# Self-attention on one core: four of sixteen key tiles a step added up by accumulating transfers instead of by TensorE and GpSimd

## The chip, the core and the metric

The kernel runs on one core of one Trainium2 chip. The metric is the device time of one execution in microseconds (us), taken as the median of several runs. One profiled execution stands beside it: it shows what each engine did, with every instruction's start and duration.

## What is computed

A transformer block pair: a cross-attention layer with residual, then a layer with self-attention, cross-attention and an MLP. The change touches the self-attention alone. Cut to that, the reference says:

```python
def mha(q, k, v):                       # B = 2, N = 2048, C = 512, 16 heads of d = 32
    scores = jnp.einsum('bqhd,bkhd->bhqk', qh, kh) / jnp.sqrt(jnp.asarray(d, q.dtype))
    attn = jax.nn.softmax(scores, axis=-1)
    out = jnp.einsum('bhqk,bkhd->bqhd', attn, vh)
    return out.reshape(B, Nq, C)

h = mha(q, k, v) @ self_o_w + self_o_b
x = x + h * gate_msa
```

All is float32 in and out. Every query's exponentials over 2048 keys have to be added up (the softmax's denominator), and this sum is what the change distributes anew.

## The kernel before

The program is a row of stages, each written by hand as one instruction list per engine with explicit semaphores: conditioning, a first cross-attention pass, the dense projections to q, k and v, the self-attention (`attention`, named a2, tiles a_...), a second cross-attention pass and the MLP. Nothing schedules it; the order is the order of the code.

The self-attention makes 32 steps: 2 batches, 4 groups of 4 heads (`GH`), 4 chunks of 512 queries (`W`). A step has 64 slots, x = 0 to 63: 16 key tiles kt of 128 keys times 4 heads. In slot x TensorE does `score_tile` (one score tile, keys on partitions, into a ring of three PSUM banks `st`), then the work that the hand-written table `products` gives to that slot, then `score_unit` (scores of a later step, queries on partitions, for their maxima). Around it:

- ScalarE takes each score tile out of `st` with an exponential into `e`, a ring of `ER` = 4 key tiles of [128 x 4 heads x 512] float32, 1 MB each. Before it writes tile kt it waits until TensorE has used the tile that stood in that place (`tile_used`) and, if GpSimd adds up that tile, until it has (`e_added`).
- VectorE takes the maximum of each `score_unit` (L1973). Once a step they are all there, it writes the negated maxima, GpSimd computes their lower parts (`lower_parts`, L2045), TensorE turns them (`turn_peaks`, L1807, in slot `TURN` - 1), ScalarE copies the rows (`take_rows`), and SP spreads them by a transfer into the next step's queries (`spread_rows`, L1738). The first score tile of the next step waits for that transfer.
- `weigh(kt)` (L1832) is four matmuls, one a head, that multiply the exponentials of key tile kt with the values and accumulate in `acc`, bank 0.
- The denominators accumulate in `acc`, bank 1, in one of two ways. A tile of `SUMMED` (3, 5, 8, 10, 15) is added by TensorE with a matrix of ones (`add_up`, four matmuls, L1841). The eleven tiles of `POOLED` are first added up element by element by GpSimd into `esum` (`add`, L2038, ten additions of 128 x 2048), and one `add_partial` (four matmuls, L1850) takes the sum in. The first addition of a step waits until TensorE is done with the sum of the step before; in before that is behind the products of slot 9.
- `fetch_sums` (ScalarE) takes both banks out, `divide` (VectorE, three parts) inverts the denominators, `scale` (GpSimd, L2051) multiplies, SP stores. The new step's `weigh(0)` waits for `fetch_sums`.

A matmul of `weigh` or of the sums is float32 in 32 columns and shows as two records of the trace, so such a call of four matmuls shows as x8. GpSimd's list for a step is: additions 1 to 7, `lower_parts` for the next step, addition 8, `scale` of the step before, additions 9 and 10. SP issues, per step: three query loads (L1720, `QR` = 4 buffers, three steps ahead), every fourth step key and value loads (L1728, L1732), the store of a finished chunk, and the spread of the rows. All transfers of the kernel before are issued by SP.

Of the kernel before, what the change touches and what calls it, by code (L numbers as in the profile page):

```python
# [13 lines left out]
P = 128  # L14
# [6 lines left out]
W = 512  # L21
# [1570 lines left out]
def attention(nc, d, name, q_in, k_in, v_in, o_out, keys, preload):  # L1592
# [30 lines left out]
    TURN = 60  # L1623
# [4 lines left out]
    DIVIDE_AT = (16, 24, 52)  # L1628
    FETCH_AT, SPREAD_AT = 9, 37
    SETUP = 2 + KW % 2  # L1630
    with nc.cleanup_on_exit(), ExitStack() as ctx:
# [12 lines left out]
        if POOLED:  # L1644
            esum = sb("esum", [P, GH, W])
        peak = sb("peak", [P, U])
# [3 lines left out]
        sums = sb("sums", [P, 2, 2, W])  # L1650
        den_t = sb("den_t", [P, W])
        inv = sb("inv", [P, W // DH])
        inv_b = sb("inv_b", [P, W])
        inv_t = sb("inv_t", [P, 2, W])
# [7 lines left out]
        score_done, score_read, tile_used, e_added = sem("score_done"), sem("score_read"), sem("tile_used"), sem("e_added")  # L1662
        divided, acc_read, scaled, spread = sem("divided"), sem("acc_read"), sem("scaled"), sem("spread")
# [120 lines left out]
        def _(pe):  # L1784
# [37 lines left out]
            def weigh(i, j, kt):  # L1822

                n, g = BODY * i + j, j // CHUNKS
                if kt == 0:
                    pe.wait_ge(acc_read, n + 1)
                    if j % CHUNKS == 0:
                        pe.wait_ge(v_loaded[g % 2], DMA * (i + g // 2 + 1))
                pe.wait_ge(score_read, number(i, j, place(kt, GH - 1)) + 3)
                for h in range(GH):  # L1830
                    rows = slice(h * DH, (h + 1) * DH)
                    mm = pe.matmul(acc[rows, 0], v[0:KR, g % 2, kt, rows], e[0:KR, (j * NKT + kt) % ER, h],  # L1832
                                   start=(kt == 0), stop=(kt == NKT - 1), tile_position=(0, h * DH))
                if kt in POOLED or kt in SUMMED_FIRST:
                    mm.then_inc(tile_used, 1)

            def add_up(i, j, kt):

                pe.wait_ge(score_read, number(i, j, place(kt, GH - 1)) + 3)
                for h in range(GH):  # L1840
                    mm = pe.matmul(acc[h * DH:(h + 1) * DH, 1], ones[0:KR], e[0:KR, (j * NKT + kt) % ER, h], start=(kt == SUMMED[0]),  # L1841
                                   stop=False, tile_position=(0, h * DH))
                if kt not in SUMMED_FIRST:
                    mm.then_inc(tile_used, 1)

            def add_partial(i, j):

                pe.wait_ge(e_added, (BODY * i + j + 1) * ADDS)
                for h in range(GH):
                    mm = pe.matmul(acc[h * DH:(h + 1) * DH, 1], ones[0:KR], esum[:, h], start=False, stop=True, tile_position=(0, h * DH))  # L1850

            def products(i, j, x):

                if x == 4 and exists(i, j - 1):
                    add_up(i, j - 1, 15)
                    weigh(i, j - 1, 14)
                elif x == 9 and exists(i, j - 1):
                    add_partial(i, j - 1)
                    weigh(i, j - 1, 15)
                elif x == 14 and exists(i, j):  # L1860
                    weigh(i, j, 0)
                elif x == 20 and exists(i, j):
                    weigh(i, j, 1)
                    weigh(i, j, 2)
                    weigh(i, j, 3)
                elif x == 25 and exists(i, j):
                    add_up(i, j, 3)
                elif x == 30 and exists(i, j):
                    weigh(i, j, 4)
                    add_up(i, j, 5)  # L1870
                    weigh(i, j, 5)
                elif x == 35 and exists(i, j):
                    weigh(i, j, 6)
                elif x == 40 and exists(i, j):
                    weigh(i, j, 7)
                elif x == 45 and exists(i, j):
                    weigh(i, j, 8)
                elif x == 50 and exists(i, j):
                    add_up(i, j, 8)
# [31 lines left out]
        def _(act):  # L1911
# [8 lines left out]
            def exponential(i, j, kt, h):  # L1920
                n = BODY * i + j
                if h == 0:
                    act.wait_ge(tile_used, n * NKT + kt + 1)
                    before = (kt - ER) % NKT
                    if before in POOLED and (kt >= ER or exists(i, j - 1)):

                        act.wait_ge(e_added, (n - (kt < ER)) * ADDS + max(POOLED.index(before), 1))
# [11 lines left out]
            def fetch_sums(i, j):  # L1939
                n = BODY * i + j  # L1940
                act.wait_ge(tile_used, (n + 1) * NKT + ER)
                act.wait_ge(scaled, n + 1)
                act.activation(sums[:, j % 2], acc[:], ACT.Copy).then_inc(acc_read, 1)
# [21 lines left out]
        def _(dve):  # L1965
# [19 lines left out]
            def divide(i, j, part):  # L1985
# [3 lines left out]
                if part == 0:  # L1989
                    dve.wait_ge(acc_read, n + 2)  # L1990
                    ins = dve.transpose(den_t[:], sums[:, j % 2, 1])
# [37 lines left out]
        def _(pool):  # L2029
# [17 lines left out]
            def scale(i, j):  # L2047
# [3 lines left out]
                pool.tensor_tensor(o[:, j % 2], sums[:, j % 2, 0], inv_t[:, j % 2], ALU.mult).then_inc(scaled, 1)  # L2051
# [256 lines left out]
```

## Time and profile before

| | us |
|---|---|
| median of 3 runs | 4050.16 (4046.61 to 4053.0) |
| the profiled execution | 4039.68 |
| its span, first to last instruction | 4037.9 |
| TensorE busy in the span | 3696.0 (92%) |
| VectorE, ScalarE, GpSimd busy | 2264.0, 1858.7, 2231.7 |
| first addition of the attention to its last `weigh` | 955.0 to 2683.3 |

A busy engine is one that has an instruction running; an idle stretch ahead of an instruction is put down to the engine or transfer that released it last. The span is cut by stage: the slices and the stretches in time order show the attention as one flat part with a period of one step. Within a step the times of the groups of TensorE and of GpSimd's additions can be subtracted from each other, and that is how the rows below are to be read.

### The profile page before, as it was taken

The page shows a single profiled execution, that of the slowest core. Times are in us where ns is not written, and L with a number is a line of the kernel's source. Part 1 is how long each engine was busy: PE and PEld are TensorE (multiplying, and loading weights), DVE is VectorE, ACT ScalarE, POOL GpSimd, SP SyncE. Part 2 cuts the span into 40 slices and gives each one's busy share as a digit, 9 for nine tenths or more (in the row PEclk, how much of TensorE's full clock was granted, in tenths as well). Part 3 has the DMA queues.
Part 4 walks back from the last instruction along what each step waited for, and adds up shares of the span by engine and source line. Part 5 has one row for each costly group of instructions (what it writes and reads, how often), then busy time and mean ns, then how long its engine had stood idle before and what let it go on. Part 6 is the DMA issues. An engine that isn't in the chain of part 4 may idle for free. (4 is left out here: it accounts for less than half of the span.)

```text
span 4037.9 us, 51412 instructions
## 1 busy us (share of the span) xinstructions
PE 3696.0 (92%) x19340; PEld 2421.3 (60%) x19340; DVE 2264.0 (56%) x3956; ACT 1858.7 (46%) x3431; POOL 2231.7 (55%) x987
## 2 busy tenths in 40 slices
PE   4699969979999999999999999958999949999998
PEld 2577748855545554555555555426777737888887
DVE  1466642228777777777777777614766634222222
ACT  1455641113666666666666666644556521111111
POOL 0356640004888888888888888864667542000000
PEclk8798889987999999999999999978999869999999
DMA  7556657773021312112131311024576651111110
GB/s 229 144 154 167 167 149 224 221 193 63 20 62 27 69 27 54 41 23 59 27 68 27 69 27 30 20 86 104 146 179 173 149 198 42 42 42 42 42 42 31
DMA packets 213509, 371.42 MB, mean 92 GB/s; under 512 B 36103, under 2 KB 52999, under 8 KB 209703
## 3 DMA queue, kind: packets, MB, share of 16 engines
q1 hardware_dynamic: 213287, 368.49, 33.6%
q8 instruction: 135, 2.21, 0.2%
q14 instruction: 87, 0.71, 0.1%
HBM read 215.54 MB, written 144.51 MB: 89 GB/s over the span
## 5 line engine op out<-in xcount | busy, mean ns | idle before, releaser
L1973 DVE TENSOR_REDUCE a_peak<-a_sm 128x1 f32<-128x512 f32 x2048 | 1263.5, 682 | 423.8 <-PE a_sm L1797 423.6
L2038 POOL TENSOR_TENSOR a_esum<-a_esum,a_e 128x2048 f32<-128x2048 f32 x288 | 1319.4, 4581 | 101.8 <-ACT a_e L1929 87.2
L1929 ACT ACTIVATE a_e<-a_st 128x512 f32<-128x512 f32 x2048 | 1063.7, 602 | 570.8 <-PE a_st L1819 476.1
L1797 PE MATMUL a_sm<-a_k,a_q 96*128 96x512 f32 x2048 | 875.6, 435 | 28.0 <-DMA a_k<-s_k 28.0
L1819 PE MATMUL a_st<-a_q,a_k 128*128 128x512 f32 x2048 | 826.3, 406 | 6.7 <-ACT a_e L1929 4.2
L1797 PEld LDWEIGHTS a_sm<-a_k,a_q 96*128 96x128 f32 x2048 | 394.3, 193 | 480.5 <-DVE a_peak L1973 267.7
L1832 PE MATMUL a_acc<-a_e,a_v 128*32 128x512 f32 x4096 | 515.7, 598 | 0.0
L1819 PEld LDWEIGHTS a_st<-a_q,a_k 128*128 128x128 f32 x2048 | 388.0, 190 | 116.7 <-ACT a_e L1929 41.6
L2169 PE MATMUL mlp_ph<-mlp_us,mlp_w_hi 128*128 128x512 f32 x1024 | 337.0, 391 | 32.6 <-DVE mlp_raw_lo L2218 32.6
L2211 ACT ACTIVATE mlp_gelu<-mlp_ph,mlp_b 128x512 f32<-128x512 f32 x128 | 88.1, 688 | 595.0 <-PE mlp_ph L2169 594.9
L2249 POOL TENSOR_TENSOR mlp_x<-mlp_x,mlp_brow 128x2048 f32<-128x2048 f32 x8 | 36.9, 4619 | 569.6 <-DMA mlp_x<-s_x 569.4
L2226 DVE CAST mlp_gs<-mlp_gelu 128x512 fp32r<-128x512 f32 x128 | 90.6, 708 | 459.2 <-ACT mlp_gelu L2211 459.2
L2184 PE MATMUL mlp_py<-mlp_w_hi,mlp_gs 128*128 128x512 f32 x1024 | 317.3, 391 | 16.7 <-DVE mlp_gs L2228 16.7
L1409 POOL TENSOR_TENSOR p_e<-p_e,p_inv 128x308 f32<-128x308 f32 x256 | 173.2, 709 | 167.1 <-DVE p_inv L1093 167.1
L1832 PEld LDWEIGHTS a_acc<-a_e,a_v 128*32 128x32 f32 x4096 | 110.2, 109 | 246.5 <-issue 159.5
L2169 PEld LDWEIGHTS mlp_ph<-mlp_us,mlp_w_hi 128*128 128x128 f32 x1024 | 193.7, 189 | 73.6 <-issue 33.0
L2184 PEld LDWEIGHTS mlp_py<-mlp_w_hi,mlp_gs 128*128 128x128 f32 x1024 | 191.6, 188 | 60.9 <-issue 16.1
L2038 POOL TENSOR_TENSOR a_esum<-a_e 128x2048 f32<-128x2048 f32 x32 | 146.9, 4591 | 130.9 <-PE a_acc L1832 115.4
L587 PE MATMUL p_sm<-p_ks,p_qs 96*128 96x78 f32 x1024 | 167.7, 306 | 50.1 <-DMA p_qs<-s_q 29.7
L587 PEld LDWEIGHTS p_sm<-p_ks,p_qs 96*128 96x128 f32 x1024 | 153.2, 217 | 82.2 <-issue 27.6
L2169 PE MATMUL mlp_ph<-mlp_us,mlp_raw_lo 128*128 128x512 f32 x512 | 200.3, 391 | 0.0
L2184 PE MATMUL mlp_py<-mlp_raw_lo,mlp_gs 128*128 128x512 f32 x512 | 199.9, 390 | 0.0
(150 smaller groups left out, 5167.7 us busy)
## 6 DMA issues: line engine op xcount, KB each, us to landing
p_qs<-s_q SPq DMA_DIRECT2D x192, 256.0 KB, 5.9
s_q<-p_qo SPq DMA_DIRECT2D x64, 512.0 KB, 7.4
a_q<-s_q SPq DMA_DIRECT2D x96, 256.0 KB, 5.2
a_k<-s_k SPq DMA_DIRECT2D x24, 1024.0 KB, 15.9
s_x<-p_x SPq DMA_DIRECT2D x16, 1024.0 KB, 4.3
s_u<-p_ut_hi SPq DMA_DIRECT2D x64, 256.0 KB, 5.8
s_u<-p_ut_lo SPq DMA_DIRECT2D x64, 256.0 KB, 6.4
p_us<-s_u SPq DMA_DIRECT2D x16, 1024.0 KB, 7.9
```

Of the source, the lines that this page charges most:

```text
L587: mm = pe.matmul(sm[:, unit % 2, h * KE:(h + 1) * KE], qs[0:3 * DH, g % 2, h, qt * P:(qt + 1) * P], ks[0:3 * DH, b, g * GH + h], start=Tru ...
L1409: pool.tensor_tensor(e[:, number % 2, qt, :, 0:S], e[:, number % 2, qt, :, 0:S], inv[:, number % 2, qt].unsqueeze(2).to_broadcast([P, GH, ...
L1797: mm = pe.matmul(sm[:, bank_of_unit(j, u), x * KE:(x + 1) * KE], q[0:3 * DH, j % QR, h, qt * P:(qt + 1) * P], k[0:3 * DH, g % 2, h, kc * K ...
L1819: pe.matmul(st[0:KR, place(kt, h) % RING], k[:, g % 2, h, kt * P:kt * P + KR], q[:, j % QR, h], start=True, stop=True).then_inc(score_done, 1)
L1832: mm = pe.matmul(acc[rows, 0], v[0:KR, g % 2, kt, rows], e[0:KR, (j * NKT + kt) % ER, h], start=(kt == 0), stop=(kt == NKT - 1), tile_posi ...
L1929: act.activation(e[0:KR, (j * NKT + kt) % ER, h], st[0:KR, place(kt, h) % RING], ACT.Exp, scale=SCALE).then_inc(score_read, 1)
L1973: dve.tensor_reduce(dst, src, AX.X, ALU.max).then_inc(unit_read, 1)
L2038: pool.tensor_tensor(esum[:], e[:, slot(0)] if x == 1 else esum[:], e[:, slot(x)], ALU.add).then_inc(e_added, 1)
L2169: mm = pe.matmul(ph[:, m % 4], w1[pw][:, t, m * P:(m + 1) * P], us[:, b, pm, t], start=(t == 0 and s == 0), stop=(t == KT - 1 and s == 2))
L2184: mm = pe.matmul(py[:, tt], gs[:, m % 2, pw, tt * P:(tt + 1) * P], w2[pm][:, m], start=(m == 0 and s == 0), stop=(m == HT - 1 and s == 2))
L2211: act.activation(gelu[:, m % 2], ph[:, m % 4], ACT.Gelu_apprx_tanh, bias=b1[:, m:m + 1]).then_inc(gelu_done, 1)
L2226: dve.tensor_copy(gs[:, m % 2, 0], gelu[:, m % 2]).then_inc(g_hi, 1)
```

## The change

The sixteen key tiles are distributed over three ways instead of two. GpSimd adds ten tiles (0, 1, 3, 4, 5, 7, 8, 10, 13, 14: nine additions), TensorE two (11 and 15), and four tiles (`MOVED`: 2, 6, 9, 12) are moved by transfers that GpSimd issues itself: tile 2 is copied from `e` to a second partial sum `esum_moved`, and 6, 9 and 12 are added to it by accumulating transfers of 1 MB each, every one waiting for the landing of the one before. A new `add_moved` (four matmuls) takes that sum in, at slot 14; GpSimd's first addition of a step now waits for it. ScalarE, before it writes a place of the ring that a moved tile held, waits for its transfer. The ring `e` grows to five tiles; to make room the query buffers go from 4 to 3, `sums` has one buffer instead of two, and `den_t` shares its place with `inv_b`. The product groups of TensorE move: ten groups, mostly six slots apart, instead of twelve, mostly five apart. The turn comes in slot 57 instead of 59, `fetch_sums` in slot 19 instead of 9, the three divisions at VectorE's 37, 48 and 51 instead of 16, 24 and 52.

```diff
-    QR = 4
-    ER = 4
-
-    POOLED = [0, 1, 2, 4, 6, 7, 9, 11, 12, 13, 14]
-    SUMMED = [3, 5, 8, 10, 15]
-    SUMMED_FIRST = [5, 10, 15]
+    QR = 3
+    ER = 5
+
+    POOLED = [0, 1, 3, 4, 5, 7, 8, 10, 13, 14]
+    MOVED = [2, 6, 9, 12]
+    SUMMED = [11, 15]
+    SUMMED_FIRST = [11, 15]
...
-    TURN = 60
+    TURN = 58
...
-    DIVIDE_AT = (16, 24, 52)
-    FETCH_AT, SPREAD_AT = 9, 37
+    DIVIDE_AT = (37, 48, 51)
+    FETCH_AT, SPREAD_AT = 19, 49
...
-                if kt in POOLED or kt in SUMMED_FIRST:
+                if (kt in POOLED or kt in MOVED or kt in SUMMED_FIRST) and kt < NKT - 1:
                     mm.then_inc(tile_used, 1)
...
+            def add_moved(i, j):
+
+                pe.wait_ge(e_moved, DMA * (BODY * i + j + 1) * len(MOVED))
+                for h in range(GH):
+                    mm = pe.matmul(acc[h * DH:(h + 1) * DH, 1], ones[0:KR], esum_moved[:, h], start=False, stop=True, tile_position=(0, h * DH))
+                mm.then_inc(tile_used, 1)
 
             def products(i, j, x):
 
-                if x == 4 and exists(i, j - 1):
+                if x == 2 and exists(i, j - 1):
+                    weigh(i, j - 1, 14)
                     add_up(i, j - 1, 15)
-                    weigh(i, j - 1, 14)
-                elif x == 9 and exists(i, j - 1):
+                    weigh(i, j - 1, 15)
+                elif x == 8 and exists(i, j - 1):
                     add_partial(i, j - 1)
-                    weigh(i, j - 1, 15)
-                elif x == 14 and exists(i, j):
+                elif x == 14 and exists(i, j - 1):
+                    add_moved(i, j - 1)
+                elif x == 22 and exists(i, j):
                     weigh(i, j, 0)
-                elif x == 20 and exists(i, j):
                     weigh(i, j, 1)
                     weigh(i, j, 2)
...
-                elif x == 55 and exists(i, j):
-                    add_up(i, j, 10)
                     weigh(i, j, 10)
+                    add_up(i, j, 11)
                     weigh(i, j, 11)
-                elif x == 63 and exists(i, j):
                     weigh(i, j, 12)
+                elif x == 60 and exists(i, j):
                     weigh(i, j, 13)
...
+                    if m >= 0 and before in MOVED:
+                        act.wait_ge(e_moved, DMA * (m * len(MOVED) + MOVED.index(before) + 1))
...
+            def move(i, j, y):
+
+                n, kt = BODY * i + j, MOVED[y]
+                pool.wait_ge(score_read, number(i, j, place(kt, GH - 1)) + 3)
+                if y == 0:
+                    pool.wait_ge(tile_used, n * NKT + ER)
+                    pool.dma_start(esum_moved[:], e[:, (j * NKT + kt) % ER]).then_inc(e_moved, DMA)
+                else:
+                    pool.wait_ge(e_moved, DMA * (n * len(MOVED) + y))
+                    pool.dma_start(esum_moved[:], e[:, (j * NKT + kt) % ER], accum_op=ALU.add).then_inc(e_moved, DMA)
 
             def step(i, j):
                 for x in range(1, len(POOLED)):
+                    if x == 2 and exists(i, j):
+                        move(i, j, 0)
+                    if x == 4 and exists(i, j):
+                        move(i, j, 1)
+                    if x == 6 and exists(i, j):
+                        move(i, j, 2)
+                    if x == 8 and exists(i, j):
+                        move(i, j, 3)
```

All the groups of `products` after the change, by slot: 2 (weigh 14, sum of 15, weigh 15), 8 (partial sum of GpSimd), 14 (moved sum), 22 (weigh 0 to 2), 28 (3), 34 (4), 40 (5 to 7), 46 (8), 52 (weigh 9 and 10, sum of 11, weigh 11 and 12), 60 (13). Before: 4 (sum of 15, weigh 14), 9 (partial sum, weigh 15), 14 (0), 20 (1 to 3), 25 (sum of 3), 30 (weigh 4, sum and weigh of 5), 35 (6), 40 (7), 45 (8), 50 (sum of 8, weigh 9), 55 (sum of 10, weigh 10 and 11), 63 (12, 13).

GpSimd's list for one step, before: the first addition of a step (from two tiles of `e`), six more, the lower parts of the maxima (`a_neg`), an addition, the scaling (`a_o`), two additions.

```order
L2038 TENSOR_TENSOR a_esum<-a_e 128x2048
L2038 TENSOR_TENSOR a_esum<-a_esum,a_e 128x2048 x6
L2045 TENSOR_TENSOR a_neg<-a_minus,a_neg 128x4x4
L2038 TENSOR_TENSOR a_esum<-a_esum,a_e 128x2048
L2051 TENSOR_TENSOR a_o<-a_sums,a_inv_t 128x512
L2038 TENSOR_TENSOR a_esum<-a_esum,a_e 128x2048 x2
```

The same list after the change:

```order
L2047 TENSOR_TENSOR a_esum<-a_e 128x2048
L2068 DMA a_esum_moved<-a_e 128x2048
L2047 TENSOR_TENSOR a_esum<-a_esum,a_e 128x2048 x2
L2071 DMA a_esum_moved<-a_e 128x2048
L2047 TENSOR_TENSOR a_esum<-a_esum,a_e 128x2048 x2
L2071 DMA a_esum_moved<-a_e 128x2048
L2047 TENSOR_TENSOR a_esum<-a_esum,a_e 128x2048 x2
L2071 DMA a_esum_moved<-a_e 128x2048
L2054 TENSOR_TENSOR a_neg<-a_minus,a_neg 128x4x4
L2047 TENSOR_TENSOR a_esum<-a_esum,a_e 128x2048
L2060 TENSOR_TENSOR a_o<-a_sums,a_inv_t 128x512
L2047 TENSOR_TENSOR a_esum<-a_esum,a_e 128x2048
```

The four transfers stand between the additions, all four ahead of the lower parts; these still come after seven additions.

TensorE from the turn to the last product group of a step, before (`a_st<-a_ident` is the turn, `a_st` a score tile, `a_sm` a unit for the maxima):

```order
L1807 MATMUL a_st<-a_ident,a_neg 128x128 x4
L1819 MATMUL a_st<-a_q,a_k 128x512
L1797 MATMUL a_sm<-a_k,a_q 128x512
L1819 MATMUL a_st<-a_q,a_k 128x512
L1797 MATMUL a_sm<-a_k,a_q 128x512
L1819 MATMUL a_st<-a_q,a_k 128x512
L1797 MATMUL a_sm<-a_k,a_q 128x512
L1819 MATMUL a_st<-a_q,a_k 128x512
L1832 MATMUL a_acc<-a_e,a_v 32x512 x8
```

And after the change:

```order
L1810 MATMUL a_st<-a_ident,a_neg 128x128 x4
L1822 MATMUL a_st<-a_q,a_k 128x512
L1800 MATMUL a_sm<-a_k,a_q 128x512
L1822 MATMUL a_st<-a_q,a_k 128x512
L1800 MATMUL a_sm<-a_k,a_q 128x512
L1822 MATMUL a_st<-a_q,a_k 128x512
L1835 MATMUL a_acc<-a_e,a_v 32x512 x4
```

The turn stands two slots further from the step's end, and the group behind it holds one call instead of two.

## Rows read from the trace of the kernel before

**Rows 1.** The page, busy tenths of TensorE in 40 equal slices of the span.

```profile
PE   4699969979999999999999999958999949999998
```

**Rows 2.** GpSimd in time order, one step: start, duration, instruction, idle before, releaser.

```profile
1714.52 4.58 POOL L2038 TENSOR_TENSOR a_esum<-a_e 128x2048 f32<-128x2048 f32 x1 [3.66 <-PE a_acc L1832]
1719.25 9.30 POOL L2038 TENSOR_TENSOR a_esum<-a_esum,a_e 128x2048 f32<-128x2048 f32 x2
1729.23 4.57 POOL L2038 TENSOR_TENSOR a_esum<-a_esum,a_e 128x2048 f32<-128x2048 f32 x1 [0.68 <-ACT a_e L1929]
1734.00 4.60 POOL L2038 TENSOR_TENSOR a_esum<-a_esum,a_e 128x2048 f32<-128x2048 f32 x1 [0.21 <-ACT a_e L1929]
1739.58 4.59 POOL L2038 TENSOR_TENSOR a_esum<-a_esum,a_e 128x2048 f32<-128x2048 f32 x1 [0.98 <-ACT a_e L1929]
1745.12 4.59 POOL L2038 TENSOR_TENSOR a_esum<-a_esum,a_e 128x2048 f32<-128x2048 f32 x1 [0.95 <-ACT a_e L1929]
1749.67 0.23 POOL L2045 TENSOR_TENSOR a_neg<-a_minus,a_neg 128x16 f32<-128x16 f32 x1
...
1754.40 1.27 POOL L2051 TENSOR_TENSOR a_o<-a_sums,a_inv_t 128x512 f32<-128x512 f32 x1
...
1768.57 4.59 POOL L2038 TENSOR_TENSOR a_esum<-a_e 128x2048 f32<-128x2048 f32 x1 [3.63 <-PE a_acc L1832]
```

**Rows 3.** One step's window: PE, PEld, DVE, ACT, POOL busy, granted clock, DMA share, GB/s.

```profile
1714.50:1768.50 54.00, 54.00 (x309) 27.15 (x309) 41.08 (x69) 35.09 (x68) 47.17 (x12) 1.00 0.10 25
```

**Rows 4.** TensorE in time order, same step: product groups, turn, next first score tile.

```profile
1716.90 1.07 PE L1832 MATMUL a_acc<-a_e,a_v 128*32 128x512 f32 x8
...
1721.04 2.78 PE L1832 MATMUL a_acc<-a_e,a_v 128*32 128x512 f32 x24
...
1726.30 1.06 PE L1841 MATMUL a_acc<-a_e,a_ones 128*32 128x512 f32 x8
...
1729.84 1.07 PE L1832 MATMUL a_acc<-a_e,a_v 128*32 128x512 f32 x8
...
1750.21 1.07 PE L1841 MATMUL a_acc<-a_e,a_ones 128*32 128x512 f32 x8
...
1755.14 0.60 PE L1807 MATMUL a_st<-a_ident,a_neg 128*128 128x128 f32 x4
...
1757.54 1.92 PE L1832 MATMUL a_acc<-a_e,a_v 128*32 128x512 f32 x16
...
1759.76 0.50 PE L1819 MATMUL a_st<-a_q,a_k 128*128 128x512 f32 x1
...
1762.07 1.06 PE L1841 MATMUL a_acc<-a_e,a_ones 128*32 128x512 f32 x8
...
1767.35 1.04 PE L1832 MATMUL a_acc<-a_e,a_v 128*32 128x512 f32 x8
```

**Rows 5.** VectorE in time order, same step: five peaks.

```profile
1733.10 3.08 DVE L1973 TENSOR_REDUCE a_peak<-a_sm 128x1 f32<-128x512 f32 x5 [2.18 <-PE a_sm L1797]
```

**Rows 6.** SP in time order: start and time that an issue holds it.

```profile
1756.46 0.61 SPq L1738 DMA_DIRECT2D a_q<-a_rows  x1
...
1759.13 0.36 SPq L1747 DMA_DIRECT2D s_o<-a_o  x1
...
1813.13 2.15 SPq L1728 DMA_DIRECT2D a_k<-s_k  x3
```

**Rows 7.** The 32 spreads of the rows (line 1738), from issue to landing.

```profile
DMA to landing us min/median/max: 3.2/3.3/5.0
```

**Rows 8.** The page's DMA issues: engine, count, KB each, median us from issue to landing.

```profile
a_k<-s_k SPq DMA_DIRECT2D x24, 1024.0 KB, 15.9
s_x<-p_x SPq DMA_DIRECT2D x16, 1024.0 KB, 4.3
...
p_x<-in_x SPq DMA_DIRECT2D x8, 1024.0 KB, 6.3
```

**Rows 9.** ScalarE in time order, same step: the fetch of the sums.

```profile
1714.41 1.03 ACT L1943 ACTIVATE a_sums<-a_acc 128x1024 f32<-128x1024 f32 x1 [1.18 <-PE a_acc L1832]
```

More of the change, by code:

```diff
@@ L1649, in attention @@
         rows = sb("rows", [P, 2, W])
-        sums = sb("sums", [P, 2, 2, W])
-        den_t = sb("den_t", [P, W])
+        sums = sb("sums", [P, 2, W])
         inv = sb("inv", [P, W // DH])
         inv_b = sb("inv_b", [P, W])
+        den_t = inv_b
         inv_t = sb("inv_t", [P, 2, W])
@@ L1849, in add_partial @@
                 for h in range(GH):
-                    mm = pe.matmul(acc[h * DH:(h + 1) * DH, 1], ones[0:KR], esum[:, h], start=False, stop=True, tile_position=(0, h * DH))
+                    mm = pe.matmul(acc[h * DH:(h + 1) * DH, 1], ones[0:KR], esum[:, h], start=False, stop=False, tile_position=(0, h * DH))
+            def add_moved(i, j):
[3 more added lines that the diff above has]
+                mm.then_inc(tile_used, 1)
@@ L1861, in products @@
                     weigh(i, j, 0)
-                elif x == 20 and exists(i, j):
                     weigh(i, j, 1)
                     weigh(i, j, 2)
+                elif x == 28 and exists(i, j):
                     weigh(i, j, 3)
-                elif x == 25 and exists(i, j):
-                    add_up(i, j, 3)
-                elif x == 30 and exists(i, j):
+                elif x == 34 and exists(i, j):
                     weigh(i, j, 4)
-                    add_up(i, j, 5)
+                elif x == 40 and exists(i, j):
@@ L1871, in products @@
                     weigh(i, j, 5)
-                elif x == 35 and exists(i, j):
                     weigh(i, j, 6)
-                elif x == 40 and exists(i, j):
                     weigh(i, j, 7)
-                elif x == 45 and exists(i, j):
+                elif x == 46 and exists(i, j):
                     weigh(i, j, 8)
-                elif x == 50 and exists(i, j):
-                    add_up(i, j, 8)
+                elif x == 52 and exists(i, j):
                     weigh(i, j, 9)
-                elif x == 55 and exists(i, j):
-                    add_up(i, j, 10)
@@ L1923, in exponential @@
                     act.wait_ge(tile_used, n * NKT + kt + 1)
-                    before = (kt - ER) % NKT
-                    if before in POOLED and (kt >= ER or exists(i, j - 1)):
-                        act.wait_ge(e_added, (n - (kt < ER)) * ADDS + max(POOLED.index(before), 1))
+                    before, m = (kt - ER) % NKT, n - (kt < ER)
+                    if m >= 0 and before in POOLED:
+                        act.wait_ge(e_added, m * ADDS + max(POOLED.index(before), 1))
+                    if m >= 0 and before in MOVED:
+                        act.wait_ge(e_moved, DMA * (m * len(MOVED) + MOVED.index(before) + 1))
                 act.wait_ge(score_done, number(i, j, place(kt, h)) + 1)
@@ L1941, in fetch_sums @@
                 act.wait_ge(tile_used, (n + 1) * NKT + ER)
-                act.wait_ge(scaled, n + 1)
-                act.activation(sums[:, j % 2], acc[:], ACT.Copy).then_inc(acc_read, 1)
+                act.wait_ge(scaled, n + 2)
+                act.activation(sums[:], acc[:], ACT.Copy).then_inc(acc_read, 1)
             def step(i, j):
@@ L1990, in divide @@
                     dve.wait_ge(acc_read, n + 2)
-                    ins = dve.transpose(den_t[:], sums[:, j % 2, 1])
+                    if n > 0:
+                        dve.wait_ge(divided, DIVIDES * n)
+                    ins = dve.transpose(den_t[:], sums[:, 1])
                 else:
```

8 lines of the change are left out of this document (5 added, 3 removed).

## The prediction

> **What bounds the kernel now.** I read the page's slices first, then one regular step of the attention in time order on each engine, then the waits. The attention is the flat stretch in the middle of the slices: TensorE at 9 tenths throughout [rows 1]. One regular step, from one first add of GpSimd to the next, lasts 1768.57 - 1714.52 = 54.05 us [rows 2], and there are 32. In a window of that length TensorE is busy all the time, at the full granted clock (1.00, its level of 2.4 GHz), GpSimd 47.17 us, VectorE 41.08, ScalarE 35.09 [rows 3]. The reader should see two things. TensorE sets the pace: it alone has no idle time in the step. But GpSimd, which this change touches most, is only some 7 us behind that: 3.63 us of idle ahead of its first add and 0.68 + 0.21 + 0.98 + 0.95 = 2.82 us ahead of later ones [rows 2].
>
> **Prices on TensorE** come from the distances between its product groups [rows 4]. A "quad" here is one call of weigh, add_up, add_partial or add_moved (four matmuls, eight records). One quad and five slots: 1729.84 - 1726.30 = 3.54 us. Three quads and five slots: 1726.30 - 1721.04 = 5.26, so a further quad is (5.26 - 3.54) / 2 = 0.86. One quad and six slots: 1721.04 - 1716.90 = 4.14, so a sixth slot costs 0.60, about VectorE's pitch (five peaks in 3.08 us, 0.62 each [rows 5]); in the five-slot runs a slot is at most (3.54 - 0.86) / 5 = 0.54. Three quads, eight slots and the turn: 1757.54 - 1750.21 = 7.33.
>
> **The change on TensorE.** It removes the sums of tiles 3, 5, 8 and 10 (four quads), adds those of tile 11 and of the moved partial (two); tile 15's stays. 22 quads in 12 groups become 20 in 10. Summed from the rows above by the new places: three stretches of three quads and six slots (from 2, 22 and 40), 3 x (4.14 + 1.72) = 17.58; five of one quad and six slots (8, 28, 34, 46, 60), 5 x 4.14 = 20.70; 14 to 22, one quad and eight slots, 4.14 + 2 x 0.60 = 5.34; 52 to 60, five quads, eight slots and the turn, 7.33 + 1.72 = 9.05. Sum 52.67: **52.7 us a step if TensorE still paces it**, 1.35 less than now. The two quads alone are 1.72; longer runs that go at VectorE's pitch give some back.
>
> **The change on GpSimd.** One add of ten goes (4.6 us), four transfers come in, which GpSimd itself issues. Its cycle now closes through TensorE at two new places: the first add waits until add_moved, at slot 14 (the last quad of group 9 before), and the turn, at slot 57 (59 before), still waits for lower_parts, behind seven adds and now four issues. Call an issue a. Round the loop:
> - first add to the end of lower_parts: now 1749.67 + 0.23 - 1714.52 = 35.38 us, less the 2.82 of waiting, 32.56 [rows 2]; plus 4a.
> - lower_parts to the turn: 0.18, the hand-over that rows show the other way, from a quad's end to GpSimd's first add (1767.35 + 1.04 to 1768.57) [rows 2, 4].
> - turn to the next step's first score tile: 1759.76 - 1755.14 = 4.62 [rows 4]. This is no TensorE time alone: ScalarE copies the rows, SP issues their spread at 1756.46, and with the median landing of 3.3 it is there at 1759.76, to the hundredth [rows 6, 7]. Six slots and one quad take about as long. Plus r, what the last move, in flight just then on the same DMA engines, adds to that landing.
> - first score tile to add_moved: slot 4's group now starts 1762.07 - 1759.76 = 2.31 after it, so slot 2's, two slots sooner, at about 1.3; then 5.86 and 4.14: 11.30. From a quad's start to GpSimd's first add: 1768.57 - 1767.35 = 1.22 [rows 2, 4].
>
> Sum 32.56 + 0.18 + 4.62 + 11.30 + 1.22 = 49.88: **49.9 + 4a + r**. GpSimd paces the step as soon as 4a + r exceeds 52.7 - 49.9 = 2.8. TensorE would then stand some 1 us a step at the turn or behind it; I take its granted clock to stay where it is.
>
> **The unknowns.** No transfer is issued by GpSimd in the trace of before. The nearest rows for a are SP's issues: 0.36 for a small store, 2.15 / 3 = 0.72 for each of three 1 MB loads [rows 6]; from above, the smallest work of size on GpSimd, 1.27 for 128x512 [rows 2]. Below zero is excluded, since an issue takes the engine. I take 0.72, the row of the same size. For r the spread's landing is 3.2 at best and 5.0 at worst [rows 7], so 0 to 1.7; I take half, 0.85. The transfers' own length D: a 1 MB store lands in 4.3, a load of 1 MB in 6.3, three queued loads in 15.9 [rows 8]; an adding transfer also fetches its target, which I estimate at twice 6.3 = 12.6 from above and 4.3 from below. Consecutive adding moves are issued two adds and one issue apart, 9.30 + 0.72 = 10.0 us [rows 2], so D below 10 hides behind the adds, and so does the slot that each move holds: with five tiles it must be free some 10 us after the issue. The first move, a plain copy, is needed back sooner, some 6 us after its issue; 4.3 to 6.3 fits.
>
> The Trainium skill ("DMA: Bandwidth & Descriptors", Latency and other measured facts) puts the first byte of a transfer issued by GpSimd at about 1 us and of one by SP at about 0.6. With a = 1 the loop would be 54.75 us and the time 4072, beyond the break-even of the dear issue below; the SP rows here agree with its second figure in size (0.36 to 0.72), and no run shows the first yet.
>
> **Edits costed at nothing.** Fewer query buffers: the load two steps ahead is issued at a step's start and needed at slot 50, some 40 us on (50/64 of a step), against a landing of 15.9 us for the longest loads of this stage [rows 8]. Fetching the sums at slot 19 takes ScalarE 1.03 us [rows 9] before weigh 0 may start in slot 22; three slots of TensorE, some 1.6 us at 0.54, hide it, and if that cover fails it is up to 1 us a step, 33 in all. One sums buffer and the later divisions: scale stands at GpSimd's last add, over 10 us behind slot 51. SP's queue gains nothing: the moves have GpSimd's own queue, but share the DMA engines, 10% busy now [rows 3].
>
> **Forecast: GpSimd paces the step, a little shorter than now.** 49.9 + 4 x 0.72 + 0.85 = 53.63 us, 0.42 less, x 32 = 13 us. The profiled execution took 4039.7 us, 1.8 above its span; 13 less is 4026.7. The median of the runs lies 10.5 above that execution, so **4037 us** there. What is won in TensorE quads is mostly spent waiting at the turn.
>
> **Rivals.**
> - TensorE still paces (a of 0.5 or less: SP's cheap issue, 0.36, gives 49.9 + 1.44 + 0.85 = 52.2, under 52.7). Gain 1.35 x 32 = 43: 4007. For it: GpSimd issues only 128 whole rows a move. Against it: nothing hides 4a, since every add waits for the one before.
> - The issue is dear, slower than before. Place: the four issues ahead of lower_parts. Price 4 us a step for each us of a; it decides from a = (54.05 - 49.9 - 0.85) / 4 = 0.83. At 1.27: 49.9 + 5.08 + 0.85 = 55.83, 1.78 more, x 32 = 57: 4107. For it: GpSimd's smallest bulk work takes that long, and SP's 0.72 is by another engine. Against: an issue moves no elements.
> - The moves are long. From D = 10.0 on, move 2 waits for move 1 and move 3 for move 2, both ahead of lower_parts. At 12.6: 2 x 2.6 = 5.2 a step, 58.83, 4.78 x 32 = 153: 4203. Against it: the DMA engines are 10% busy.
> - It does nothing measurable: a near 0.83, within the forecast's own spread.
>
> **Chances and range.** Forecast (a of 0.5 to 0.83) 0.36, with its own range 4008 to 4050; TensorE paces 0.25; dear issue 0.27; long moves 0.10; 0.02 for something else. A difference under 0.2% (8 us: 4042 to 4058) can't be told from no change here. Faster: 0.25 + 0.21 of the forecast's share = 0.46; within 0.2%: its other 0.15 and the 0.02, 0.17; slower: 0.27 + 0.10 = 0.37. Range: from 3990, TensorE pacing with 0.5 us a step less than summed (the fourteen slots beyond five would give 0.8 at 0.54 instead of 0.60, and behind three quads VectorE has run dry), to 4115, just over the dear issue at 1.27. Left out: the long moves and little below.
>
> **What the profile after would show.** Step length between two first adds, against 53.6. The gap between two adds with a move between them less 4.55 is a. TensorE's idle at the turn put down to a_neg (some 1 us a step), and at the first score tile to a_q<-a_rows (r); with neither, TensorE paces. Waits of an add or an exponential for a move's landing mean long moves. I am wrong on mechanism if the step's wait ends elsewhere: at slot 28 on the first move, or in weigh 0 behind the later fetch.

## The result: 2.4% slower

The changed kernel takes 4147.25 us (median of 4 runs, 4140.34 to 4152.14) against 4051.19 of the kernel before, measured beside it: a ratio of 1.0241, 95% interval 1.0222 to 1.0260. All ratios here are of fast runs; one execution of early_split below, 8195.57 us at a granted clock of 0.42, was in the slow state and is left out of its numbers. Forecast was 4037, in a range from 3990 to 4115. The step of the attention did not fall from 54.05 to 53.6 us, it rose to 57.5 us.

### The profile after

First the page: TensorE's slices and its granted clock, the second DMA queue, which is new, and the score tiles' group with its idle time (columns of that row: busy time, mean ns, then idle time before and what ended it).

```profile
PE   4699969979999999999999999975999959999998
...
PEclk8798879978999999999999999986999969999999
...
q0 software_dynamic: 18432, 134.23, 14.2%
...
L1822 PE MATMUL a_st<-a_q,a_k 128*128 128x512 f32 x2048 | 831.1, 408 | 94.2 <-DMA a_q<-a_rows 85.8
```

The slices can hardly be told from [rows 1]: a step that loses under 3 us in 57 still shows a 9. What gives it away is the last row: TensorE now stands 85.8 us in the program ahead of score tiles, until the spread of the rows has landed. That wait is the first one to follow.

GpSimd in time order over one step, as [rows 2] (start, duration, instruction, idle before, releaser). Line numbers have moved: additions are L2047, the copying move L2068, the adding moves L2071, the lower parts L2054.

```profile
1764.73 4.61 POOL L2047 TENSOR_TENSOR a_esum<-a_e 128x2048 f32<-128x2048 f32 x1 [9.83 <-PE a_acc L1859]
1769.27 0.58 POOL L2068 DMA_DIRECT2D a_esum_moved<-a_e  x1
1769.87 9.35 POOL L2047 TENSOR_TENSOR a_esum<-a_esum,a_e 128x2048 f32<-128x2048 f32 x2
1779.16 0.89 POOL L2071 DMA_DIRECT2D a_esum_moved<-a_e  x1
1779.78 9.63 POOL L2047 TENSOR_TENSOR a_esum<-a_esum,a_e 128x2048 f32<-128x2048 f32 x2
...
1799.47 0.88 POOL L2071 DMA_DIRECT2D a_esum_moved<-a_e  x1
1800.07 0.54 POOL L2054 TENSOR_TENSOR a_neg<-a_minus,a_neg 128x16 f32<-128x16 f32 x1
...
1822.27 4.60 POOL L2047 TENSOR_TENSOR a_esum<-a_e 128x2048 f32<-128x2048 f32 x1 [11.44 <-PE a_acc L1859]
```

From first add to first add it is 57.54 us. Between the first add and the lower parts there is no idle time left; ahead of the first add there are 9.83 and 11.44 us of it, waiting for `add_moved`. An issue holds GpSimd from 1769.27 to 1769.87, 0.60, and from 1779.16 to 1779.78, 0.62 (the recorded 0.89 overlaps the addition behind it).

TensorE in the same step, as [rows 4]: the turn, the next step's first score tile, the groups behind it and `add_moved`.

```profile
1800.67 0.66 PE L1810 MATMUL a_st<-a_ident,a_neg 128*128 128x128 f32 x4 [0.28 <-POOL a_neg L2054]
...
1805.00 0.39 PE L1800 MATMUL a_sm<-a_k,a_q 96*128 96x512 f32 x1
1808.06 0.50 PE L1822 MATMUL a_st<-a_q,a_k 128*128 128x512 f32 x1 [2.67 <-DMA a_q<-a_rows]
...
1809.27 0.63 PE L1822 MATMUL a_st<-a_q,a_k 128*128 128x512 f32 x1
1809.83 1.94 PE L1835 MATMUL a_acc<-a_e,a_v 128*32 128x512 f32 x8
...
1821.03 1.06 PE L1859 MATMUL a_acc<-a_esum_moved,a_ones 128*32 128x512 f32 x8
```

SP's issue in that step, as [rows 6], with what the trace says of all 32 spreads (as [rows 7]: who waited, us and times, then minimum, median and maximum to landing).

```profile
1802.04 0.60 SPq L1741 DMA_DIRECT2D a_q<-a_rows  x1
...
  PE a_st L1822: 85.8, 31
...
DMA to landing us min/median/max: 3.4/6.0/7.5
```

The spread is issued 1.37 us behind the turn, as it was before (1.32 [rows 4, 6]), but lands 6.0 us later instead of 3.3. It has company: the fourth move was issued at 1799.47, 2.57 us ahead of it, and the adding moves take 7.3 us to land. Of the moves the trace gives, in the same three numbers, first line 2068 (the copy), then line 2071 (the adding ones):

```profile
DMA to landing us min/median/max: 4.5/4.7/11.2
...
DMA to landing us min/median/max: 6.9/7.3/9.2
```

The last rows that matter are windows, as [rows 3] (busy time of PE, PEld, DVE, ACT, POOL, then granted clock, DMA share, GB/s): the same step in whole, the stretch of the turn and the wait, the spread from issue to first score tile in this trace and then in that of the kernel before, and the 6 us behind the first score tile of the step before this one and of this one.

```profile
1764.73:1822.27 57.54, 54.60 (x293) 26.63 (x293) 41.21 (x69) 35.71 (x67) 45.66 (x15) 0.97 0.42 96
1800.00:1808.00 8.00, 5.12 (x26) 2.74 (x25) 5.40 (x9) 4.51 (x9) 8.00 (x5) 1.00 0.89 182
...
1802.04:1808.06 6.02, 3.35 (x18) 1.60 (x17) 3.56 (x6) 3.14 (x6) 6.02 (x3) 1.00 0.98 201
...
1756.46:1759.76 3.30, 3.30 (x21) 1.09 (x20) 1.87 (x4) 2.06 (x4) 3.30 (x1) 1.00 0.59 124
...
1752.12:1758.12 6.00, 6.00 (x37) 3.01 (x38) 2.66 (x5) 2.71 (x6) 2.78 (x1) 1.00 0.54 148
1808.06:1814.06 6.00, 6.00 (x30) 2.13 (x31) 1.37 (x2) 1.68 (x3) 2.77 (x1) 0.72 0.62 151
```

Two things are to be seen. While the spread is under way the DMA engines are busy 0.98 of the time, where the same stretch before the change had 0.59 (the 0.10 of [rows 3] is the mean of a whole step). And behind TensorE's idle stretch of 2.67 us its granted clock is 0.72 over 6 us, part of it at the lower of its two levels (1.2 instead of 2.4 GHz): a score tile takes 0.63 us instead of 0.40, a product call 1.94 instead of 1.07. It is not so every time. The step before waited 2.69 us at the same place and kept 1.00. Of the 31 steps that waited, 5 kept the full clock over these 6 us, and 26 show 0.51 to 0.73.

The same two rows of TensorE in that step before, first score tile and `add_moved`:

```profile
1752.12 0.50 PE L1822 MATMUL a_st<-a_q,a_k 128*128 128x512 f32 x1 [2.69 <-DMA a_q<-a_rows]
...
1763.49 1.06 PE L1859 MATMUL a_acc<-a_esum_moved,a_ones 128*32 128x512 f32 x8
```

They are 11.37 us apart, with the clock down 12.97.

So the step has two new losses, one behind the other: TensorE waits for the spread, and then mostly runs slowly for a while. From first add to first add 31 steps take 57.57 us on the mean instead of 54.12, which is 107 of the 110.8 us that the profiled execution is longer.

### The profile page after: what moved, and what is told of

It is laid out like the page before. It is cut to its first block and busy times, and to the rows that moved or that the text cites. A ratio compares the mean times of both kernels' runs of the same rounds, so it can differ in the third digit from the quotient of the medians.

```text
span 4148.7 us, 50612 instructions
## 1 busy us (share of the span) xinstructions
PE 3706.2 (89%) x18828; PEld 2405.3 (58%) x18828; DVE 2263.7 (55%) x3956; ACT 1874.6 (45%) x3431; POOL 2183.3 (53%) x1083
## 5 line engine op out<-in xcount | busy, mean ns | idle before, releaser
L1936 ACT ACTIVATE a_e<-a_st 128x512 f32<-128x512 f32 x2048 | 1075.8, 599 | 675.6 <-PE a_st L1822 546.0
L2047 POOL TENSOR_TENSOR a_esum<-a_esum,a_e 128x2048 f32<-128x2048 f32 x256 | 1204.8, 4706 | 17.7 <-ACT a_e L1936 3.3
L1800 PE MATMUL a_sm<-a_k,a_q 96*128 96x512 f32 x2048 | 903.9, 448 | 28.3 <-DMA a_k<-s_k 28.3
L1822 PE MATMUL a_st<-a_q,a_k 128*128 128x512 f32 x2048 | 831.1, 408 | 94.2 <-DMA a_q<-a_rows 85.8
L1835 PE MATMUL a_acc<-a_e,a_v 128*32 128x512 f32 x4096 | 526.9, 622 | 0.4 <-ACT a_sums L1950 0.4
L2047 POOL TENSOR_TENSOR a_esum<-a_e 128x2048 f32<-128x2048 f32 x32 | 147.1, 4597 | 366.7 <-PE a_acc L1859 351.2
```

Of the source, the lines that this page charges most:

```text
L1800: mm = pe.matmul(sm[:, bank_of_unit(j, u), x * KE:(x + 1) * KE], q[0:3 * DH, j % QR, h, qt * P:(qt + 1) * P], k[0:3 * DH, g % 2, h, kc * K ...
L1822: pe.matmul(st[0:KR, place(kt, h) % RING], k[:, g % 2, h, kt * P:kt * P + KR], q[:, j % QR, h], start=True, stop=True).then_inc(score_done, 1)
L1936: act.activation(e[0:KR, (j * NKT + kt) % ER, h], st[0:KR, place(kt, h) % RING], ACT.Exp, scale=SCALE).then_inc(score_read, 1)
L2047: pool.tensor_tensor(esum[:], e[:, slot(0)] if x == 1 else esum[:], e[:, slot(x)], ALU.add).then_inc(e_added, 1)
```

## Experiments

The first theory is this chain: the traffic of the last move delays the spread, and the idle stretch that follows costs clock. Its first rival is the one that the prediction gave most room among the losses, the time that GpSimd spends issuing. Another is that key loads, not moves, are in the spread's way. Ratios are against the kernel before on the same chip; a step is the distance of two first adds.

### The moves without their bytes (small_moves)

```diff
-                    pool.dma_start(esum_moved[:], e[:, (j * NKT + kt) % ER], accum_op=ALU.add).then_inc(e_moved, DMA)
+                    pool.dma_start(esum_moved[:, 0, 0:16], e[:, (j * NKT + kt) % ER, 0, 0:16], accum_op=ALU.add).then_inc(e_moved, DMA)
```

The copying move is cut in the same way, and `esum_moved` is set to zero once ahead of the attention, so most of four tiles is left out of the denominators. The number of issues, their places and all waits stay.

> Each of the four moves of a step carries 16 elements a partition instead of 2048 (8 KB in all instead of 1 MB), so the denominators lack most of four tiles; the four issues, their waits and the order stay. Theory 1 (the last move is in flight on the DMA engines when SP's spread of the rows is issued, the spread lands in 6.0 us instead of 3.3, TensorE idles 2.7 us at the step's first score tile, and its granted clock falls behind that): the spread lands in 3.3 to 3.5 us again, no idle time at the first score tile, clock 1.00, a step of 52.7 to 53.3 us, time 4010 to 4030. Rival A (what GpSimd spends on four issues and their place ahead of the lower parts sets the step): issues cost as much, the step stays at 57 us, time about 4145.

Measured: 4027.5 us in one run, a step of 53.35, the clock 1.00 throughout the attention. The spread's landings and GpSimd's issues:

```profile
DMA to landing us min/median/max: 3.2/3.2/3.6
...
1796.07 0.85 POOL L2072 DMA_DIRECT2D a_esum_moved<-a_e  x1
1796.68 0.51 POOL L2055 TENSOR_TENSOR a_neg<-a_minus,a_neg 128x16 f32<-128x16 f32 x1
```

With four issues of the same length (1796.07 to 1796.68, 0.61) and no bytes worth speaking of, the 4 us a step are gone. Not the issues, the bytes cost the time.

### The idle stretch filled (fill)

To see the clock by itself, TensorE computes the last unit of a step eleven times instead of once, in the very stretch in which it would wait. The repeats write the same values to the same place.

```diff
-                        score_unit(i, *units[x])
+                        score_unit(i, *units[x], times=11 if x == GH * NKT - 1 else 1)
```

> The last score unit of a step (slot 63) is computed eleven times over into the same bank, so that TensorE works through most of the 2.7 us in which it waits for the spread; nothing else changes, the output is the same. Theory 1 with its second half (the idle stretch drops the granted clock to its lower level for some 4 us, which costs 1.6 us a step): the spread lands as late as before (6.0 us), but the granted clock stays at 1.00 in the stretch behind it; a step of 55.5 to 56 us instead of 57.1, time 4095 to 4110. Rival B (the clock falls for another reason, or its fall costs nothing since the step waits elsewhere): the step stays at 57 us or gets longer, time 4145 to 4160.

Measured: 4131.3 us, ratio 1.0224 (1.0207 to 1.0241). TensorE at the end of one step:

```profile
1795.25 2.67 PE L1800 MATMUL a_sm<-a_k,a_q 96*128 96x512 f32 x11
1798.24 0.50 PE L1822 MATMUL a_st<-a_q,a_k 128*128 128x512 f32 x1 [0.32 <-DMA a_q<-a_rows]
```

The spread lands as late as after the change (median 6.0), and the wait for it is now 0.32 behind work instead of 2.67 of idleness. An ordinary step is 55.9, 1.6 less. Four of the five steps of the changed kernel that kept the full clock have the same length (55.86 to 55.95 from first add to first add; the fifth is the first step, 57.86). Where the gap is still long the clock still falls: behind the waits of 1.8 to 2.5 us that remain it is 0.50 to 0.73, behind all those under 1.5 us it is 1.00. So the idle stretch takes the clock, and this costs 1.6 us a step. The total is a miss: the ratio stands 0.0017 under that of the change, half the width of either interval, and 4131 is not the 4095 to 4110 expected. Several steps are longer than 55.9, up to 60.8. Part of the reason is in the trace: in the six later steps with key loads ScalarE waits 3.3 to 3.7 us for the copying move, against 1.7 to 2.9 after the change, and they take 58.1 on the mean; three other steps, of 58.9 to 60.8, are among those in which a long wait and a fallen clock remain. What makes the spread so late in those, these runs don't tell.

### The turn ahead of the last move (early_turn)

The lower parts are computed one addition sooner, so ahead of the fourth move, and the turn comes four slots sooner.

```diff
-    TURN = 58
+    TURN = 54
...
-                    if x == 8 and exists(i, j + 1):
+                    if x == 7 and exists(i, j + 1):
```

> The lower parts come one addition sooner in GpSimd's list (ahead of addition 7) and the turn four slots sooner (slot 53 instead of 57); all moves stay. Theory 1: the spread may land as late, but has four more slots, some 2 to 2.5 us, and is issued ahead of the last move; TensorE's idle time at the first score tile all but goes, the clock stays at 1.00, and TensorE paces the step at 52.7 to 53.3 us, time 4010 to 4030, below both kernels. Rival A (four issues in GpSimd's loop) would also gain by the addition taken out ahead of the lower parts, to about the same; rival C (the moves slow TensorE or ScalarE elsewhere, through the ring's places) leaves the step above 54.5 and the time above 4065.

Measured: 4073.68 us, ratio 1.0081 (1.0064 to 1.0098). Most steps are 52.9, as expected of a step that TensorE paces; the spread lands in 3.7 (median) and is hidden. It is not issued ahead of the last move, as expected, but together with it, here SP's spread and GpSimd's fourth move of one step:

```profile
1277.60 0.60 SPq L1741 DMA_DIRECT2D a_q<-a_rows  x1
...
1277.60 0.90 POOL L2071 DMA_DIRECT2D a_esum_moved<-a_e  x1
```

In the ordinary steps of this kernel and of early_split the two issues are within 0.1 us of each other, and the adding move costs the spread 0.3 to 0.4 us. In the changed kernel the spread comes 2.55 us behind it and loses 2.7. What makes the difference between these two distances no run here shows.

But every fourth step, the one with SP's key loads, takes 59.4 to 63.0, and this is a second loss that the expectation did not have. One such step, ScalarE first, then GpSimd, then SP:

```profile
1194.90 2.08 ACT L1936 ACTIVATE a_e<-a_st 128x512 f32<-128x512 f32 x4 [4.65 <-DMA a_esum_moved<-a_e]
...
1184.59 0.60 POOL L2068 DMA_DIRECT2D a_esum_moved<-a_e  x1
...
1195.36 0.89 POOL L2071 DMA_DIRECT2D a_esum_moved<-a_e  x1 [0.87 <-DMA a_esum_moved<-a_e]
...
1214.68 0.24 POOL L2054 TENSOR_TENSOR a_neg<-a_minus,a_neg 128x16 f32<-128x16 f32 x1 [3.72 <-DVE a_minus L1990]
...
1169.61 2.40 SPq L1731 DMA_DIRECT2D a_k<-s_k  x3
1180.01 0.38 SPq L1735 DMA_DIRECT2D a_v<-s_v  x1
```

SP issues 3 MB of keys at 1169.61 and 1 MB of values at 1180.01, GpSimd its first move at 1184.59. That copy, 4.6 us on the median, is not landed 10 us later: ScalarE, which needs the tile's place in the ring, stands 4.65 us, the next move 0.87, and the maxima and the lower parts of this step are late in their turn (3.72). In the changed kernel ScalarE waits for the copy too, 1.7 to 2.9 us in the same six steps, but there it costs nothing that shows: these steps take 57.6 on the mean, like all others.

### Three moves instead of four (tile12_pe)

Tile 12 is added by TensorE, so that no move stands between the seventh addition and the lower parts.

```diff
-    MOVED = [2, 6, 9, 12]
-    SUMMED = [11, 15]
-    SUMMED_FIRST = [11, 15]
+    MOVED = [2, 6, 9]
+    SUMMED = [11, 12, 15]
+    SUMMED_FIRST = [11, 12, 15]
...
+                    add_up(i, j, 12)
...
-                    if x == 8 and exists(i, j):
-                        move(i, j, 3)
```

> Tile 12 is added up by TensorE again (one quad more, in the group of slot 52), so the last of the four moves goes; the other three and the output stay. Theory 1: with no move in flight at the spread it lands in 3.3 us, no idle time at the first score tile, and TensorE paces at 52.7 + 0.86 = 53.6 us, time 4030 to 4045. Rival A (GpSimd's issues): one issue of 0.6 us less a step, 56.5 us, time about 4128.

Measured: 4061.44 us in one run. An ordinary step is 53.7, as expected; the spread lands in 3.2 again. The steps with key loads are 58.3 to 60.3, the same second loss as in early_turn, and it takes all that the others win.

### The early turn with the loads spread out (early_split)

For the second loss the theory is that the copying move queues behind the key and value loads; so SP is given one key load a step and the value load in the fourth.

```diff
-                if j % CHUNKS == 0 and exists(i, j + CHUNKS):
-                    load_k(i, j // CHUNKS + 1)
...
+                if exists(i, (j // CHUNKS + 1) * CHUNKS):
+                    if j % CHUNKS < 3:
+                        load_k(i, j // CHUNKS + 1, j % CHUNKS)
+                    else:
...
+                        load_v(i, j // CHUNKS + 1)
```

The turn is that of early_turn.

> early_turn, and the next group's loads taken apart: one of the three 1 MB key loads in each of the first three steps of a group and the value load in the fourth, instead of all four in the first. Theory 2 (behind the late spread stands a second cost: in every fourth step 4 MB of key and value loads on the same DMA engines hold up the first move, ScalarE waits for it before tile 7, and that step takes 62.8 us instead of 52.9): all steps take 52.9 to 53.3 us, 1.1 less than in the kernel before, and the time is 0.989 to 0.994 of the kernel before's, 4000 to 4020 where that is 4042. Rival D (those steps are long for their own work, not for the loads in flight): they stay over 60 us and the ratio stays at 1.008.

Measured: 4019.42 us (median of 5), ratio 0.9937 (0.9923 to 0.9951): **0.6% faster than the kernel before**, the interval clear of 1, and so faster than the changed kernel too. The spread's and the copying move's landings, and a window of one step:

```profile
DMA to landing us min/median/max: 3.4/3.6/8.2
...
DMA to landing us min/median/max: 4.5/4.6/6.1
...
1740.00:1793.00 53.00, 52.91 (x296) 26.13 (x292) 41.03 (x69) 35.54 (x67) 45.81 (x16) 1.00 0.54 125
```

The copy's longest landing is 6.1 instead of 11.2, and all steps are 52.9 but three: the first (59.84; 54.77 before), the last (54.60; 53.06), and the one in which the second batch begins (57.22; 54.35), where TensorE waits 2.79 us for a spread that lands late. TensorE is busy 52.91 of 53.00 us at the full clock, with the same four moves a step. 1.13 us a step would be 36 us in 32 steps; the runs show 25. The three odd steps, beside the same ones before, take 5.1, 1.5 and 2.9 back. So it stands in the profile too: the fetch of the last sums, first in early_split and then in the kernel before, comes 1702.79 us behind the first add instead of 1729.07, 26 less.

```profile
2663.50 1.02 ACT L1952 ACTIVATE a_sums<-a_acc 128x1024 f32<-128x1024 f32 x1 [11.55 <-PE a_acc L1861]
...
2684.12 1.02 ACT L1943 ACTIVATE a_sums<-a_acc 128x1024 f32<-128x1024 f32 x1 [11.10 <-PE a_acc L1832]
```

The spans of the two profiled executions are only 16 apart: the first add comes at 960.71 instead of 955.05, and 4.4 us are lost behind the attention. The first lies within what the ten kernels here show at this place (953.58 to 962.76); what the second is, the profiles don't tell.

### The loads spread out alone (split_k)

The same edit of SP's loads without the early turn.

```diff
-                    load_k(i, j // CHUNKS + 1)
...
+                        load_k(i, j // CHUNKS + 1, j % CHUNKS)
```

> The changed kernel with the same loads taken apart, the turn left where it is. Theory 1 and 2: the spread still lands in 6.0 us and ordinary steps stay at 57.5 us; only the steps with key loads lose their 1 to 1.5 us. Ratio 1.018 to 1.024. If the key loads were what holds up the spread in all steps (rival E), steps drop under 55 us and the ratio under 1.01.

Measured: 4140.83 us, ratio 1.0252 (1.0235 to 1.0269). An ordinary step is 57.5, the spread lands in 6.0 as before the edit, and the wait for it is 84.5 us instead of 85.8. Key loads are not in the spread's way: that rival falls. The expectation had a small gain, from steps with key loads that it took to be 1 to 1.5 us longer than the others. In the changed kernel they are not (57.6 on the mean), so there was nothing of that kind to win, and the ratio is that of the change within both intervals.

### The last move as a plain copy (last_plain)

Same place, same tile, same megabyte, but copied instead of added.

```diff
-                    pool.dma_start(esum_moved[:], e[:, (j * NKT + kt) % ER], accum_op=ALU.add).then_inc(e_moved, DMA)
+                    pool.dma_start(esum_moved[:], e[:, (j * NKT + kt) % ER], **({} if y == 3 else dict(accum_op=ALU.add))).then_inc(e_moved, DMA)
```

> The last of the four moves is a plain copy instead of an adding one (the denominators lose the three tiles moved before); its issue, size and place stay. Adding moves land in 7.3 us and the plain first one in 4.7. Theory 1, by the bytes in flight: the spread, issued some 2 us behind that move, lands in 4.0 to 4.7 us instead of 6.0, TensorE waits about 1 us less than half as long, its clock stays up, and an ordinary step takes 54.3 to 55.2 us. If it is the transfer's issue by GpSimd, and not its length, that holds up the spread (rival F), the landing stays at 6.0 and the step at 57.5.

Measured: 4051.11 us in one run. An ordinary step is 53.69, less than the expected 54.3 to 55.2; the steps with key loads keep the second loss (57.2 to 58.8). The spread's wait and landings, and one wait on TensorE:

```profile
  PE a_st L1822: 16.2, 21
...
DMA to landing us min/median/max: 3.2/3.9/5.5
...
1710.78 0.50 PE L1822 MATMUL a_st<-a_q,a_k 128*128 128x512 f32 x1 [0.57 <-DMA a_q<-a_rows]
```

A copy in flight at the same place costs the spread 0.6 to 0.7 us (3.9 against 3.2 or 3.3), an adding transfer 2.7. So most of the delay comes with the adding; that its longer stay in flight (7.3 against 4.7) is the reason fits, but no run separates the two. 0.85, the prediction's value for r, would have been about right for a plain copy.

### Three moves and the loads spread out (tile12_split)

tile12_pe and the loads of split_k together.

```diff
-    MOVED = [2, 6, 9, 12]
+    MOVED = [2, 6, 9]
...
+                        load_k(i, j // CHUNKS + 1, j % CHUNKS)
```

> tile12_pe (tile 12 added up by TensorE, three moves) with the key and value loads taken apart. Theory 1 and 2 together: every step at 53.7 us, as the ordinary steps of tile12_pe, 0.35 less than in the kernel before: ratio 0.996 to 0.999. Rival D: the long steps stay, ratio 1.005.

Measured: 4029.32 us, ratio 0.9963 (0.9949 to 0.9977). All regular steps are 53.7, those with loads too. With early_split this is the second kernel in which both losses are taken away, the first of them by another means, and both come out ahead of before (here by 0.4%); the step differs by the quad of tile 12 (0.86 in the prediction's price list): 53.7 - 52.9 = 0.8.

## Why the prediction was wrong, step by step

The loop was the right one: GpSimd's first add, its additions and issues, the turn, the spread, and TensorE up to `add_moved`. The four legs, predicted and measured in the step shown above:

| leg | predicted us | measured us | by |
|---|---|---|---|
| first add to the turn, with four issues | 35.62 | 35.94 | 1764.73 to 1800.67 |
| turn to first score tile, with r | 5.47 | 7.39 | 1800.67 to 1808.06 |
| first score tile to `add_moved` | 11.30 | 12.97 | 1808.06 to 1821.03 |
| `add_moved` to first add | 1.22 | 1.24 | 1821.03 to 1822.27 |
| step | 53.6 | 57.54 | |

- **The issue, a = 0.72: near enough.** It is 0.60 to 0.62. The rival that I gave 0.27, a dear issue, fell on its price; small_moves shows the same. It put the slower side into the chances, but for a reason that did not happen. The Trainium skill ("DMA: Bandwidth & Descriptors", Latency and other measured facts) gives about 1 us to the first byte of a transfer that GpSimd issues, and the prediction set that figure beside a. It is no price for GpSimd's own time: 0.60 us after an issue's start GpSimd is at its next addition. The SP rows of 0.36 to 0.72 are no first byte either, but the time that an issue holds SP. When a first byte moves no run here shows.
- **r = 0.85: this step failed.** It is 7.39 - 4.62 = 2.77. I took its bound from the spread's own landings, 3.2 to 5.0 [rows 7], in a trace whose DMA engines were 10% busy over a step [rows 3] and had no 1 MB move in flight beside the spread, and so bounded the contention by rows that did not have it. The rows for it were there: a load of 1 MB in 6.3 and three queued ones in 15.9 [rows 8] hint at what it is to stand behind another transfer. I used them for the moves' own length and not for what comes behind them. I also noted that a move of under 10 us "hides behind the adds"; it does, for GpSimd, but the last one is in flight just when SP issues the one transfer that TensorE waits for. The Trainium skill states that transfers of different issuing engines run on the same sixteen DMA engines and interleave ("DMA: Bandwidth & Descriptors", Issuing engines are not separate DMA queues); the spread's landing agrees, 6.0 us behind an adding move of GpSimd and 3.3 without one. The prediction named the shared engines too, and still priced them at half of a range that had no move in it.
- **"I take its granted clock to stay where it is": this failed too,** and it is most of the 12.97. The idle stretch was forecast (some 1 us) and costed at its own length. In 26 of 31 steps it is followed by a clock of 0.51 to 0.73 over 6 us, here 0.72, and the leg behind it is 1.67 longer. In the step before, with a wait as long and the clock at 1.00, this leg takes 1763.49 - 1752.12 = 11.37, near the forecast. Of the 3.93 us between 53.6 and 57.54, r makes 1.92, the clock 1.67, and 0.32 is the rest of the additions. fill measures the clock apart from r: 1.6.
- **TensorE at 52.7 a step: right.** early_turn and early_split run at 52.9, with TensorE busy all the time; the sum of [rows 4] was 0.2 short.
- **What was costed at nothing** held, mostly. No engine waited for a query load; the fetch of the sums at slot 19 ([rows 9]; 1.06 us now) held TensorE 0.4 us in the whole program. The ring's fifth tile does not cover everything: ScalarE waited 19.0 us, 14 times, for a move, 18.7 of it for the copying one and most of that behind key loads. Here the prediction had it that "4.3 to 6.3 fits"; with 4 MB of loads ahead of it it is up to 11.2. In the changed kernel that hides behind the greater loss, and it comes out as soon as that one is gone (early_turn, tile12_pe).
- **The long moves**, at 0.10 the other slow rival, did not come either: 7.3 is under the 10.0 from which they would have queued.

The list of signs at the prediction's end served well: "at the first score tile to a_q<-a_rows (r)" is where the loss shows. The price, not the place, was missed, and the clock was left out of it.

What stays open: why 2 of 28 steps keep the clock behind an idle stretch as long as in the others, why fill's total gains less than its ordinary steps (only in part by the copying move), and why a spread issued together with an adding move loses so much less than one issued 2.55 us behind it.

## What to carry to other kernels

A transfer that costs its issuer little still takes the DMA engines for its whole flight. Before adding bulk transfers, list the short ones that an engine waits for, see what will be in flight when each of them is issued, and bound the delay from rows in which transfers do stand behind each other; then place the bulk so that none is issued just ahead of a short one on the critical path. An idle stretch put into a TensorE that had none is to be costed twice, once for its length and once for the clock behind it; here that was 2.7 us and, in 26 of 31 steps, another 1.6. And when one loss has been found, look for the next that it covered: here the same change was 2.4% slower, 0.8% slower and 0.6% faster as one and then the other was taken away.

## What the runs showed of the hardware

- An accumulating transfer of 1 MB within SBUF lands in 7.3 us, a copy of the same tile in 4.7 (7.6 and 4.6 in early_split). The first holds up a 256 KB transfer issued some 2.5 us behind it by 2.7 us, the second by 0.6 to 0.7. An adding one issued within 0.1 us of it holds it up by 0.3 to 0.4 (early_turn, early_split).
- An issue by GpSimd takes 0.6 us from its start to the next instruction's, for either kind, whether it moves 1 MB or 8 KB (16 elements in each of 128 partitions).
- Idle stretches of 2.3 to 4.3 us on a TensorE that was otherwise busy were followed in 26 of 28 cases by a granted clock of 0.51 to 0.73 over the next 6 us; the three shorter waits of this kernel (0.86, 1.66, 1.90) by 1.00. In fill a wait of 1.80 was followed by 0.72, one of 1.48 by 1.00.
- With transfers well placed, 0.55 of DMA time in the whole attention (1000 to 2500 us, early_split) costs TensorE next to nothing: its clock there is 1.00 and it is busy 1492.87 of 1500 us, against 1498.32 before at 0.19 of DMA time.
